# A four-layer graph network on one core: graph stage with broadcast targets, leaky relu and subtraction as passes of their own, exponential on the way out of PSUM

## What is computed

```python
h = jnp.einsum('bnd,ade->bane', feat_in, W)
th = jnp.tanh(h)
attn_src = jnp.einsum('bane,aeo->bano', th, w_src)
attn_dst = jnp.einsum('bane,aeo->bano', th, w_dst)
attn = attn_src + jnp.swapaxes(attn_dst, 2, 3)
attn = jnp.where(attn >= 0, attn, LEAKY_ALPHA * attn)
attn = jnp.where(mask, jnp.float32(-999.0), attn)
attn = jax.nn.softmax(attn, axis=-1)
feat_out = jnp.einsum('banm,bame->bane', attn, h) + b
feat_out = jax.nn.elu(feat_out)          # after the heads are put side by side
gate = jax.nn.sigmoid(feat_in @ H_w.T + H_b)
return gate * feat_out + (1.0 - gate) * feat_in
```

## Time and profile before

| | us |
|---|---|
| median of 3 runs | 2708.63 |
| lowest, highest | 2702.85, 2709.47 |
| profiled execution | 2709.26 |
| its span | 2707.5 |
| TensorE busy, share of the span | 2640.9 (98%) |
| VectorE | 2417.2 (89%) |
| ScalarE | 2346.9 (87%) |
| GpSimd | 1804.9 (67%) |

### The profile page before, as it was taken

One profiled execution on the slowest core, in us unless ns is written; L12 is line 12 of the kernel. 1 busy time (PEld: TensorE's weight loads), 2 busy tenths in 40 slices (PEclk: granted clock), 3 DMA queues, 4 the chain that ended last, 5 costly groups with the idle time before them and its releaser, 6 DMA issues. The chain is left out here.

```text
span 2707.5 us, 66704 instructions
## 1 busy us (share of the span) xinstructions
PE 2640.9 (98%) x20128; PEld 2385.9 (88%) x20128; DVE 2417.2 (89%) x7209; ACT 2346.9 (87%) x6600; POOL 1804.9 (67%) x1550
## 2 busy tenths in 40 slices
PE   8999999999998999999999999999999999999996
PEld 7888888888887999999999999899999999999995
DVE  6998998898887999999999999899999999999995
ACT  7999999999998888888888888888888888888884
POOL 3777766766765677766666677766666666667665
PEclk9999999999999999999999999999999999999998
DMA  3011111111104888887778888878778887878775
GB/s 99 28 38 40 33 34 39 33 33 39 37 29 130 256 260 259 263 253 252 247 252 255 256 262 264 252 255 251 253 242 259 256 250 254 253 245 257 250 249 176
DMA packets 386754, 500.42 MB, mean 185 GB/s; under 512 B 58464, under 2 KB 349152, under 8 KB 386272
## 3 DMA queue, kind: packets, MB, share of 16 engines
q1 hardware_dynamic: 386400, 496.16, 58.2%
HBM read 219.24 MB, written 201.33 MB: 155 GB/s over the span
## 5 line engine op out<-in xcount | busy, mean ns | idle before, releaser
L794 ACT ACTIVATE probs<-logits,nmax 128x256 f32<-128x256 f32 x1152 | 571.8, 500 | 104.5 <-DVE turned_sb L1072 99.6
L570 POOL TENSOR_TENSOR probs<-probs,recs 128x1024 f32<-128x1024 f32 x288 | 545.9, 1896 | 107.8 <-DVE recs L1064 107.6
L1072 DVE STREAM_TRANSPOSE turned_sb<-probs 128x512 f32<-128x512 f32 x576 | 610.7, 1103 | 4.0 <-POOL probs L570 4.0
L1051 DVE CUSTOM_DVE_ANT_0 logits<-s,mask 128x256 f32<-128x256 f32 x1152 | 430.8, 420 | 84.1 <-PE s L1456 81.4
L548 POOL TENSOR_TENSOR residual<-x,br 128x384 f32<-128x384 f32 x192 | 191.0, 1017 | 455.9 <-DVE mix L1083 455.8
L787 ACT ACTIVATE stack<-split 64x768 fp32r<-64x768 f32 x576 | 484.8, 842 | 3.4
L76 PE MATMUL pj<-xt_hi,w_lo 128*128 128x256 f32 x1728 | 481.9, 279 | 0.8 <-DVE xt_lo L1036 0.8
L78 PE MATMUL pj<-xt_hi,w_hi 128*128 128x256 f32 x1728 | 481.0, 278 | 0.0
L77 PE MATMUL pj<-xt_lo,w_hi 128*128 128x256 f32 x1728 | 480.8, 278 | 0.0
L665 ACT ACTIVATE g_exps<-g_v,g_nmax 128x256 f32<-128x256 f32 x768 | 385.3, 515 | 3.0 <-DVE g_nmax L961 0.7
L779 ACT ACTIVATE split<-pj,bc 128x256 fp32r<-128x256 f32 x576 | 239.6, 467 | 163.2 <-PE pj L78 107.3
(11 more groups left out here) (118 smaller groups left out, 7401.3 us busy)
## 6 DMA issues: line engine op xcount, KB each, us to landing
turned<-turned_sb SPq DMA_DIRECT2D x288, 512.0 KB, 5.0
pt_copy<-turned SPq DMA_DIRECT2D x288, 512.0 KB, 4.6
stack<-split SPq DMA_DIRECT2D x576, 128.0 KB, 4.4
y<-out SPq DMA_DIRECT2D x128, 384.0 KB, 5.2
x<-y SPq DMA_DIRECT2D x96, 384.0 KB, 3.1
x<-x SPq DMA_DIRECT2D x32, 384.0 KB, 3.0
adj<-adj SPq DMA_DIRECT2D x128, 64.0 KB, 3.1
w_whole<-att_w SPq DMA_DIRECT2D x24, 192.0 KB, 2.9
```

Source lines behind the costliest of these rows:

```text
L570: pool.tensor_tensor(probs[:, heads, :, :].rearrange("p h t n -> p (h t) n"), probs[:, heads, :, :].rearrange("p h t n -> p (h t) n"), rec ...
L794: last = act.activation(probs[:, (HEADS * u + h) % 4, t, :], logits[:, h % 2, t, :], ACT.Exp, scale=-1.0, bias=nmax[:, u, h, t:t + 1], acc ...
L1051: last = dve.tensor_tensor_reduce(out=logits[:, h % 2, t, :], in0=s_ps[h % 2][:, t, :], in1=mask[u][:, t, :], scale=-HEAD_DIM ** -0.5, sca ...
L1072: last = dve.transpose(turned_sb[b][:, :, :].rearrange("p k (z h q) -> p k z h q", z=NT, h=2 * NT)[:, :, kt], probs[:, 2 * b:2 * b + 2, :, ...
```

## The change

Only the graph stage changes, and the order at the seam.

- `g_make_sd` is three float32 products in place of nine, and holds minus the targets (the sign by `g_rows_of_sd`). SyncE writes the twelve rows of targets to HBM (`g_lay_rows`, 12 KB) and reads them back into all 128 partitions (`g_spread`, three DMAs of 512 KB a sample). VectorE turns the sources into columns (`g_turn_rows`).
- The scores of TensorE go. ScalarE makes source plus target and the leaky relu in one (`g_leaky`: two instructions of 128x256 a head, out of SBUF, with the source as a bias of one value per partition). The mask is laid in PSUM once a sample (`g_lay_mask`).
- `g_maximum` is as before, but takes the mask from that one tile. A new pass subtracts the maximum: of even heads on VectorE (two `tensor_scalar` a head), of odd heads on GpSimd (one `tensor_tensor`).
- TensorE transposes these logits (`g_transpose_logits`), and `g_exp` is the copy out of PSUM, 128x512, one a head. The copies `g_even_pt` and `g_odd_pt` go. Sums are made by TensorE (`g_sums_of_four`, as large as the contexts of four heads, in front of each), copied by ScalarE, turned in `g_make_back`, and inverted per tile.
- The pipeline is deeper: heads 7 to 11 of a sample are transposed in the slot behind, and elu, gate and layer norm come two slots behind (`old`). Eight tiles `g_v` hold the logits.

```diff
+        def g_v_of(u, h):
+            k = (GAT_HEADS * u + h) % g_V_BUFS
+            return (g_v_sb, g_v_more)[k // g_HALF_V][:, k % g_HALF_V, :, :]
...
+        def g_targets_ready(eng, half, u, h):
+            eng.wait_ge(g_targets_spread[u][h * g_PARTS // GAT_HEADS], 16 * (half + 1))
+            eng.wait_ge(g_sources_turned, at(1, half, u, 1))
+            eng.wait_ge(g_transposed, earlier(GAT_HEADS, half, u, h + 1 - g_V_BUFS))
...
+            def g_lay_rows(half, u):
+                held(sp, g_rows_ready, at(1, half, u, 1), passed)
+                sp.dma_start(targets_dram[u], g_rows[g_TARGETS, :]).then_inc(g_rows_laid, 16)
+            def g_spread(half, u, i):
+                sp.wait_ge(g_rows_laid, 16 * (2 * half + u + 1))
+                held(sp, g_leaky_done, earlier(GAT_HEADS, half, u, -GAT_HEADS), passed)
+                heads = slice(i * GAT_HEADS // g_PARTS, (i + 1) * GAT_HEADS // g_PARTS)
+                sp.dma_start(g_targets[u][:, heads, :], targets_dram[u, heads, :].rearrange("h n -> (h n)").partition_broadcast(P).rearrange("p (h n) -> p h n", n=N)).then_inc(g_targets_spread[u][i], 16)
+            def g_slot(far, nxt, cur, prev, old, done):
+                if cur:
+                    g_spread(*cur, 1)
+                    g_spread(*cur, 2)
+                if far:
+                    g_load_next(*far)
+                if nxt:
+                    g_lay_rows(*nxt)
+                    g_spread(*nxt, 0)
+                if old:
+                    g_store(*old)
...
+            def g_subtract(half, u, h):
+                v = g_v_of(u, h)
+                pool.wait_ge(g_maxed, at(GAT_HEADS, half, u, h + 1))
+                pool.tensor_tensor(v, v, g_nmax[:, u, h, :].unsqueeze(2).to_broadcast([P, NT, N]), ALU.subtract).then_inc(g_odd_shifted, 1)
...
-            def g_relu(half, u, h):
-                act.wait_ge(g_scores, at(GAT_HEADS, half, u, h + 1))
-                act.wait_ge(g_exped, at(GAT_HEADS, half, u, h - 2))
-                act.activation(g_v_sb[:, h % 3], s_ps[h % 2][:, :, :], ACT.Relu, scale=-0.8).then_inc(g_lrelu, 1)
+            def g_leaky(half, u, h):
+                g_targets_ready(act, half, u, h)
+                for t in range(NT):
+                    last = act.activation(g_v_of(u, h)[:, t, :], g_targets[u][:, h, :], ACT.Prelu, scale=-1.0,
+                                          bias=g_source[u][:, t, h:h + 1], alpha=LEAKY)
+                last.then_inc(g_leaky_done, 1)
             def g_exp(half, u, h):
-                act.wait_ge(g_maxed, at(GAT_HEADS, half, u, h + 1))
-                act.wait_ge(g_transposed, at(GAT_HEADS // 2, half, u, h // 2 - 1))
-                for t in range(NT):
-                    last = act.activation(g_exps[:, h % 4, t, :], g_v_sb[:, h % 3, t, :], ACT.Exp, scale=-1.0,
-                                          bias=g_nmax[:, u, h, t:t + 1], accum_out=g_sums[:, u, h, t:t + 1])
-                last.then_inc(g_exped, 1)
-            def g_even_pt(half, u, pair):
-                act.wait_ge(g_transposed, at(GAT_HEADS // 2, half, u, pair + 1))
-                act.wait_ge(g_contexts, at(g_GROUPS, half, u, pair // 2 - 1))
-                act.activation(g_pt_sb[:, g_pt_slot(u, 2 * pair)], pt_ps[0][:, :, :], ACT.Identity).then_inc(g_pt_even_read, 1)
...
+            def g_rows_of_sd(half, u):
+                ps = pj_ps[g_SD_BANK]
+                act.wait_ge(g_sd_made, at(1, half, u, 1))
+                act.wait_ge(g_sources_turned, at(1, half, u, 0))
+                if (half, u) != first:
+                    act.wait_ge(g_rows_laid, 16 * (2 * half + u))
+                act.activation(g_rows[:, :], ps[:, 0:N], ACT.Identity, scale=g_sel[:, g_SIGN]).then_inc(g_rows_ready, 1)
...
+            def g_slot(far, nxt, cur, prev, old, done):
+                if prev:
+                    g_exp(*prev, 6)
+                if old:
+                    g_elu_exp(*old)
+                if prev:
+                    g_exp(*prev, 7)
+                    g_exp(*prev, 8)
+                if cur:
+                    g_leaky(*cur, 0)
+                if prev:
+                    g_exp(*prev, 9)
+                if cur:
+                    g_leaky(*cur, 1)
+                    g_gate_tanh(*cur, 0)
+                    g_leaky(*cur, 2)
+                if prev:
+                    g_exp(*prev, 10)
+                    g_copy_ct(*prev, 1)
+                    g_exp(*prev, 11)
+                if cur:
                     g_gate_tanh(*cur, 1)
+                    g_leaky(*cur, 3)
                     g_exp(*cur, 0)
+                    g_leaky(*cur, 4)
+                    g_leaky(*cur, 5)
+                if nxt:
+                    g_state(*nxt, 0)
...
+            def g_turn_rows(half, u):
+                dve.wait_ge(g_rows_ready, at(1, half, u, 1))
+                for q in range(BLOCKS):
+                    rows = slice(q * BLOCK, (q + 1) * BLOCK)
+                    last = dve.transpose(g_source[u][rows, :, :], g_rows[rows, :].rearrange("p (t q n) -> p t q n", t=NT, q=BLOCKS)[:, :, q, :])
+                last.then_inc(g_sources_turned, 1)
+            def g_invert_sums(half, u, t):
+                dve.wait_ge(g_back_made, at(NT, half, u, t + 1))
+                rows = g_back_bank(half, t)[:, D:D + P].rearrange("p (i e) -> p e i", e=GAT_DIM)
+                dve.reciprocal(g_recs[:, u, :, t].rearrange("p (g i) -> p g i", i=g_QUAD), rows[:, 0:g_GROUPS, :]).then_inc(g_sums_inverted, 1)
...
             def g_maximum(half, u, h):
-                held(dve, g_lrelu, at(GAT_HEADS, half, u, h + 1), passed)
+                v = g_v_of(u, h)
+                dve.wait_ge(g_mask_laid, at(1, half, u, 1))
+                held(dve, g_leaky_done, at(GAT_HEADS, half, u, h + 1), passed)
                 for t in range(NT):
                     last = dve.tensor_tensor_reduce(
-                        out=g_v_sb[:, h % 3, t, :], in0=s_ps[h % 2][:, t, :], in1=g_v_sb[:, h % 3, t, :], scale=-1.0,
+                        out=v[:, t, :], in0=s_ps[0][:, t, :], in1=v[:, t, :], scale=-1.0,
                         scalar=BIG, op0=ALU.add, op1=ALU.min, accum_out=g_nmax[:, u, h, t:t + 1])
                 last.then_inc(g_maxed, 1)
...
+            def g_subtract(half, u, h):
+                v = g_v_of(u, h)
+                dve.wait_ge(g_maxed, at(GAT_HEADS, half, u, h + 1))
+                for t in range(NT):
+                    last = dve.tensor_scalar(v[:, t, :], v[:, t, :], g_nmax[:, u, h, t:t + 1], None, ALU.subtract)
+                last.then_inc(g_even_shifted, 1)
+            def g_slot(far, nxt, cur, prev, old, done):
+                if prev:
+                    g_subtract(*prev, 8)
+                    g_maximum(*prev, 11)
+                    g_subtract(*prev, 10)
+                if old:
+                    g_elu(*old)
+                if nxt and nxt != first:
+                    g_split_x(*nxt, 0)
+                if old:
+                    g_gated_elu(*old)
                 if cur:
                     g_maximum(*cur, 0)
                     g_maximum(*cur, 1)
+                    g_subtract(*cur, 0)
+                    g_maximum(*cur, 2)
+                if nxt and nxt != first:
+                    g_split_x(*nxt, 1)
...
+                    last = pe.matmul(pj_ps[g_SD_BANK][:, 0:N], g_sd[:, c, :], g_tt[:, c, :], start=c == 0, stop=c == DC - 1)
...
+            def g_lay_mask(half, u):
+                pe.wait_ge(g_mask_ready, at(1, half, u, 1))
+                pe.wait_ge(g_maxed, at(GAT_HEADS, half, u, 0))
+                if (half, u) == first:
+                    pe.wait_ge(g_consts_ready, 1)
+                pe.matmul(s_ps[0][:, :, :], g_ident_r[:, :], g_mask[u][:, :, :], start=True, stop=True).then_inc(g_mask_laid, 1)
+            def g_transpose_logits(half, u, h):
+                v = g_v_of(u, h)
+                pe.wait_ge((g_even_shifted, g_odd_shifted)[h % 2], at(GAT_HEADS // 2, half, u, h // 2 + 1))
+                pe.wait_ge(g_exped, at(GAT_HEADS, half, u, h - 1))
                 for t in range(NT):
-                    last = pe.matmul(s_ps[h % 2][:, t, :], g_z_left[u][:, t * P:(t + 1) * P], g_z_right[u][:, h, :], start=False, stop=t == NT - 1)
-                last.then_inc(g_scores, 1)
-            def g_pair_of_transposes(half, u, pair):
-                for i in range(2):
-                    h = 2 * pair + i
-                    pe.wait_ge(g_exped, at(GAT_HEADS, half, u, h + 1))
-                    pe.wait_ge(g_pt_read[i], g_evictions(half, u, h - 2))
-                    for t in range(NT):
-                        for kt in range(NT):
-                            last = pe.transpose(pt_ps[i][:, kt, t * P:(t + 1) * P], g_exps[:, h % 4, t, kt * P:(kt + 1) * P], ident[:, :])
+                    for kt in range(NT):
+                        last = pe.transpose(pt_ps[h % 2][:, kt, t * P:(t + 1) * P], v[:, t, kt * P:(kt + 1) * P], ident[:, :])
                 last.then_inc(g_transposed, 1)
```

(117 more changed lines are left out.)

749 lines of the change are left out of this document (311 added, 438 removed).

## The result

The changed kernel takes **2859.4 us** (2858.3 to 2861.0), the kernel before, beside it, 2706.4: a ratio of 1.057, 95% interval 1.055 to 1.059. The forecast was 2758, within 2686 to 2806. It went the way that was forecast and three times as far: +153 us against +50. The profiled execution spans 2857.5 us.

The account below looks back on a forecast made before the run. ScalarE and TensorE were full; after the change, engine order was to decide. Profiled 2709.3 us, plus 31 x (26.6 - 25.1) = 46.5, minus 2 for the first slot, plus 5 at the seam: 2758.8, median 2758, range 2686 to 2806.

Parts of the forecast that it names:

- The bound and the place: Steady slot: engine order decides; TensorE waits 2.0 us ahead of the state's first product for VectorE's split of x.
- leaky pieces: ScalarE's 24 leaky relu instructions of 128x256 a sample, taken at .40 us each, 9.6 us together.
- the spreads of targets: Broadcast DMAs of targets: a rival had them late for the first leaky relu, 27.9 us a slot, 2799 us; chance .06.
- exclusion: VectorE and GpSimd holding each other up for whole instructions on shared SBUF ports, in the subtractions on the slot's chain.
- the walk: One steady slot followed through the engines' in-order lists, without VectorE and GpSimd holding each other up: 24.8 us.
- the holding-up: VectorE's and GpSimd's subtractions delaying each other: 0 to 2.5 us on the second chain, taken as +1.8, giving 26.6 a slot.
- its fall as a rival: TensorE waits 4.5 us in one piece each slot and its clock falls: some 1.7 us a slot more, 2811 us; chance .09.
- a wait of 2.0: TensorE, ready for the state at 7.0 us in the slot, waits 2.0 us for VectorE's split, done at 9.0.
- VectorE's sum: VectorE's work per slot, 21 us with some 5 of being held up, is 26, said to agree with 26.6.
- The first rival: Engines hold each other up less, or where others wait anyway: 24.8 us a slot, 2701 us; chance .30.
- the engines' sums say 22.7: Work per sample summed engine by engine: none exceeds TensorE's 22.7 us, so the order decides.

Follow-up runs that it names:

- e10_fill18: Changed kernel with one-SBUF-input subtractions on VectorE, mask laid later, and 18 unread products in TensorE's wait for the split of x: 2745.8 us, ratio 1.011.
- e11_fill9: Changed kernel with one-SBUF-input subtractions on VectorE, mask laid later, and 9 unread products in TensorE's wait for the split of x: 2746.0 us, ratio 1.012.
- e2_fill: Changed kernel with 24 unread products of 384 columns put in TensorE's wait for the split of x: 2806.4 us, ratio 1.035.
- e3_split: Changed kernel with VectorE's split of the second half of the next x moved ahead of maxima 0 to 2 and subtraction 0: 2714.0 us, ratio 1.001.
- e5_nopool: Changed kernel with GpSimd's subtractions of the odd heads left out but for one element a row: 2746.7 us, ratio 1.013.
- e9_twice: Changed kernel with every group of sums made twice on TensorE, 3.0 us more of TensorE a sample: 2877.7 us, ratio 1.060.
- e1_psum: Changed kernel with VectorE's subtractions as two-input instructions, second input the mask in PSUM, and the mask laid behind head 10: 2800.1 us, ratio 1.033.

## Why the prediction was wrong

**The bound and the place: right.** TensorE waits ahead of the first product of the state, released by VectorE's split; ScalarE is busy 68%, not the bound; leaky pieces are .40 apart; the spreads of targets land in 6.2 us and nobody waits for them. Without exclusion and with the clock held, the walk's 24.8 us is what is left of the measured 26.2 (e10_fill18, e11_fill9) when the 1.4 that the edit itself adds are taken off.

A slot came out 3.55 us longer than forecast. Two steps failed.

**The first is the holding-up, taken at +1.8 us a slot: 1.6 of the 3.55.** With the clock held (e2_fill) a slot is 28.2: 28.2 - 24.8 = **3.4 us**. Where the step looked it was nearly right: against the walk's .50 a pair, head 0 costs 1.3 more and head 10, whose meeting with GpSimd's head 11 the text names, .8, together 2.1, within the priced 0 to 2.5. It left out the others. Subtraction 8 stood in the walk at its free length: it costs .1 more, and 1.45 on top in the 12 slots in which GpSimd splits weights, a piece of work that the prediction names nowhere. Head 6 (1.48) makes TensorE wait .26 of its own. In 200 to 700 us, with 8 such slots of 17, that is 1.3 + .8 + .1 + .7 + .26, or 3.2 of the 3.4. All six pairs meet GpSimd somewhere: VectorE's subtractions are busy 131.1 us in 500, 7.9 a sample, against 6 x .55 where they meet nothing.

**The second failed step, 2.0 of the 3.55 and so the larger, is to leave the clock at nothing in the sum and to price its fall as a rival.** It had a chance of .09, as a case by itself, with a wait of 4.5 us for which no mechanism was named. But the walk gave a wait of 2.0, and the exclusion lengthens just that wait. Behind 417 us, where head 8 is hardly held up, 2.0 + 1.3 + .8 + .1 is 4.2, and 4.7 was measured; of the missing .5, .3 is the walk's own error in this place (e11_fill9), and the rest is open. Head 8's 1.45 isn't in the wait, since it holds up TensorE as well. The clock then costs 2.0 us (priced: 1.7). 24.8 + 3.4 + 2.0 = 30.2 adds up by the way in which the terms were measured; what stands by itself is the 3.2 read from the trace, and the walk. The range, up to 2806, reaches just to the larger holding-up alone (e2_fill: 2806.4), but not to the forecast with the clock's 2.0 added (some 2820), nor to both.

**A check that agreed by chance.** VectorE's sum, "21 with some 5 of being held up", was to confirm 26.6. The 5 was about right (7.9 less 3.3 is 4.6), but in the changed kernel VectorE is busy 24.7 of 30.15 us and doesn't bound; it does in e3_split.

**The first rival** (no exclusion on the path) was refuted: a subtraction takes .41 without GpSimd's subtractions and .70 with them (e5_nopool), and a slot is 28.2 us with the clock held, not 24.8. (Its sum, 2701, is 1 us low: 2708.6 - 9.3 + 3 is 2702.) The prediction's sentence that the engines' sums say 22.7 was right and of no use: e9_twice shows how little TensorE's sum counted, e3_split how much two lines of VectorE's order did.

By the Trainium skill, "SBUF — State Buffer", section "SBUF: two separate sides", whichever starts first, a two-port or two-SBUF-input instruction of VectorE or one of GpSimd, has the shared ports for its whole length, and the other is blocked. The trace agrees: .41 to .48 with one input in PSUM, against .33 to 1.13 for the `tensor_scalar` from SBUF to SBUF. It shows that a `tensor_scalar` with one value per partition is among those that are held up, which the prediction had left open.

## What to carry to other kernels

Where an engine must wait anyway, price what lengthens that wait and what follows from its length together, as one case. A pass that is cheap by itself (.28 us an instruction) can take up to four times as long (1.13) beside another engine's pass; count every such meeting on the chain, not the worst one, and also with work that runs in a part of the slots only. And before a costly rebuild is given up, look for the one instruction in an in-order list that the waiting engine needs, and move it ahead of work that nobody waits for yet: here that was worth 145 us.

## What the runs showed of the hardware

Whether TensorE's clock fell behind a wait, and for how long, varied from slot to slot at one length of the wait. Granted clock, read behind each wait of 200 to 700 us:

| kernel | wait, us | slots in which it fell to .50 |
|---|---|---|
| changed | 4.7 to 4.8 | all 17 |
| e1_psum | 3.5 to 3.7 | all 18 |
| e9_twice | 3.3 to 4.0 | 14 of 16 |
| e5_nopool | 2.6 to 3.0 | 13 of 19 |
| e11_fill9 | 1.2 to 1.5 | none |
| e3_split | .8 to .9 | none |

In e5_nopool the six microseconds behind two waits of 2.57 us, in slots next to each other:

```profile
431.70:437.70 6.00, 6.00 (x47) 0.72 0.25 76
458.30:464.30 6.00, 5.98 (x56) 1.00 0.29 81
```

In e1_psum the clock was low for 6 us behind one wait of 3.65 us, so that a part of the contexts ran slow too, and for less behind the next:

```profile
424.70:427.80 3.10, 3.05 (x10) 0.50 0.00 0
427.80:431.70 3.90, 3.90 (x38) 0.60 0.42 118
```
```profile
453.70:456.80 3.10, 3.07 (x13) 0.68 0.00 0
456.80:460.70 3.90, 3.90 (x40) 0.81 0.39 118
```

In the mean a slot lost about as much by it in e1_psum (54 us, 1.8 a slot) as in the changed kernel (2.0), though the wait was over 1 us shorter. Between 1.5 and 2.6 us nothing was tried.
